# A differential-attention layer as one sequence of 128 heads: projections and norms beside the heads, both halves of the weighing together, max pieces behind them

## What is computed

```
q1, q2, k1, k2, v = heads(x, Wq1), ...          # 16 heads, 16 wide; v 32 wide
att1 = softmax(where(mask, q1 k1^T * scale, -inf))
att2 = softmax(where(mask, q2 k2^T * scale, -inf))
y = (att1 - lam * att2) v                        # per head, causal
yn = normalise y of a head and feature over time, times gn_w, plus gn_b, times gamma
out = yn Wc^T ;  x = layernorm(x + out)
```

## Time and profile before

| | us |
|---|---|
| median of 3 runs | 6893.02 (6890.95 to 6894.93) |
| the profiled execution | 6894.07 |
| its span on the core | 6892.3 |
| TensorE busy | 6310.0 (92%) |
| VectorE, ScalarE, GpSimd busy | 4158.6, 3497.0, 817.9 |
| granted TensorE clock, mean | 0.959 |

### The profile page before, as it was taken

The page is one execution under the profiler, slowest core; times in us unless marked ns, Lnnn a source line. Parts: engine busy times, 40 slices in busy tenths (PEclk is TensorE's granted clock), DMA queues, the critical chain, the costliest instruction groups (busy, mean ns, idle before and its releaser), DMA issues.

```text
span 6892.3 us, 112906 instructions
## 1 busy us (share of the span) xinstructions
PE 6310.0 (92%) x33280; PEld 2525.2 (37%) x33280; DVE 4158.6 (60%) x10732; ACT 3497.0 (51%) x6948; POOL 817.9 (12%) x1937
## 2 busy tenths in 40 slices
PE   8989999899998989989799999999999999999985
PEld 2222232223223232232244444444444444444441
DVE  5747667475675757657565565565565565556543
ACT  4646546465564645646445445544544545544532
POOL 2222122222221212222100000000000000000000
PEclk9999999999999999999899999999999999999997
DMA  2312222232222322223100000000000000000004
GB/s 58 55 38 50 44 46 49 40 53 44 46 43 47 54 42 48 38 50 54 62 10 7 13 13 7 13 13 7 13 28 10 10 13 10 10 13 10 10 7 149
DMA packets 134759, 228.62 MB, mean 33 GB/s; under 512 B 40348, under 2 KB 40476, under 8 KB 133504
## 3 DMA queue, kind: packets, MB, share of 16 engines
q1 hardware_dynamic: 134272, 222.83, 15.6%
HBM read 53.86 MB, written 33.55 MB: 13 GB/s over the span
## 4 chain that ended last, share of the span: by engine, by line
PE 71%; DVE 10%; ACT 8%; issue 8%; DMA 2%; DVEq 1%; SPq 0%; POOL 0%; ACTq 0%; POOLq 0%
PE ps L582 16%; PE ps L664 10%; PE ps L549 9%; PE ps L788 6%; PE ps L564 4%; PE ps L813 4%; PE ps L538 4%; PE ps L715 3%; PE ps L754 3%; PE ps L735 2%; ACT pt L973 2%; PE ps L723 2%; PE ps L534 2%; ACT gates L1097 1%; DVE rr L1386 1%
## 5 line engine op out<-in xcount | busy, mean ns | idle before, releaser
L973 ACT ACTIVATE pt<-ps 128x1024 f32<-128x1024 f32 (+7 forms) x2048 | 1220.2, 650 | 923.8 <-PE ps L564 921.1
L582 PE MATMUL ps<-pt,vs 128*32 128x512 f32 (+3 forms) x6144 | 1304.1, 507 | 13.1 <-POOL pt L1594 9.3
L1234 DVE CUSTOM_DVE_ANT_0 junk<-ps,causal 128x128 bf16<-128x128 f32 (+3 forms) x2048 | 981.4, 488 | 535.7 <-PE ps L549 414.7
L582 PE MATMUL ps<-pt,ones 128*32 128x512 f32 (+3 forms) x6144 | 1304.4, 507 | 0.0
L549 PE MATMUL ps<-kt,qt 96*128 96x512 bf16 (+3 forms) x3072 | 1012.1, 337 | 134.8 <-DVE mc L1234 79.5
L1238 DVE TENSOR_REDUCE mc<-ps 128x1 f32<-128x512 f32 x1024 | 705.4, 689 | 232.9 <-PE ps L549 211.4
L564 PE MATMUL ps<-qt,kt 98*128 98x512 bf16 (+3 forms) x3072 | 770.8, 335 | 36.4 <-ACT pt L973 33.1
L549 PEld LDWEIGHTS ps<-kt,qt 96*128 96x128 bf16 x3072 | 297.5, 97 | 1265.2 <-DVE mc L1234 890.2
L664 PE MATMUL ps<-wqkv,xs 128*128 128x512 f32 x1536 | 740.5, 615 | 13.5 <-DMA wqkv<-in_wqkv 13.5
L1054 ACT ACTIVATE sm<-sm,mxw 128x256 f32<-128x256 f32 (+1 forms) x1024 | 496.7, 486 | 430.6 <-DVE mxw L1394 430.2
L1594 POOL TENSOR_SCALAR_AFFINE_SELECT pt<-pt 128x256 f32<-128x256 f32 x1024 | 423.0, 413 | 1969.2 <-ACT pt L973 1969.2
(11 more groups left out here) (144 smaller groups left out, 7869.6 us busy)
## 6 DMA issues: line engine op xcount, KB each, us to landing
qt<-part SPq DMA_DIRECT2D x768, 64.0 KB, 2.4
kt<-part SPq DMA_DIRECT2D x768, 64.0 KB, 2.6
ya<-wy SPq DMA_DIRECT2D x128, 128.0 KB, 2.3
yb<-wy SPq DMA_DIRECT2D x128, 128.0 KB, 2.4
xs<-between_phases SPq DMA_DIRECT2D x32, 512.0 KB, 3.8
between_phases<-xo SPq DMA_DIRECT2D x32, 512.0 KB, 2.8
xt<-in_x SPq DMA_DIRECT2D x8, 1024.0 KB, 5.0
between_phases<-yb SPq DMA_DIRECT2D x16, 512.0 KB, 3.6
```

The lines of the kernel that those rows point to most:

```text
L582: mmi = pe.matmul(ps[32 * q:32 * q + 32, 4 + half, lo - half * 512:hi - half * 512], w, pt[:, kb % 2, i, lo:hi], start=kb == 0, stop=kb == ...
L973: act.activation(pt[:, kb % 2, i, kb * P:1024], ps[:, 2 * i:2 * i + 2, :].rearrange("p a q -> p (a q)")[:, kb * P:1024], ACT.Exp, scale=SC ...
L1234: ins = dve.tensor_tensor_reduce(out=junk[:, bank - 6, 0:w], in0=ps[:, bank, 0:w], in1=causal[:, 512 - w:512], scale=1.0, scalar=NEG, op0= ...
```

## The change

The loop over batches and the loop over groups of heads are gone in the first phase. All 128 heads (`ALL`) are one straight sequence, and pieces of head g + 2 stand beside head g across batches too. What stood between two batches' heads is spread over heads. The function `EXTRA` tells which two results (e = 0, 1) head h of batch b carries beside it: heads 6 to 9 and 14 to 16 the q/k projections of the next batch (two tiles each), heads 10 to 13 its value projections, head 1 the last two q/k tiles of its own batch, heads 2 and 3 the output projection of the batch before, head 4 its means, head 5 its variances and divisions (counted from 1; h counts from 0). PE computes result e in key block 3 + e, in two parts with a max piece behind each, into bank 2e, which scores leave free from block 4 on. The four-head groups are summed and their statistics taken in every fourth head. Value projections are now 128 columns wide (`project_v`: four key blocks by two halves of the features, 128 features a call). `xt` is double, `yb` a quarter.

In a key block, both halves of the weighing now follow each other, and pieces stand behind the scores and behind the halves: `BESIDE` is replaced by `BESIDE_S` (behind scores 0 and 1) and `BESIDE_V` (behind each half). `copy_out` of the first half moves from block 5 to 6. The diff, cut to its core:

```diff
-BESIDE = (4, 4, 3, 3, 3, 2, 2, 3)
+BESIDE_S = ((1, 1), (1, 1), (1, 1), (0, 1), (0, 1), (0, 1), (0, 1), (1, 1))
+BESIDE_V = ((0, 2), (0, 2), (0, 1), (0, 1), (1,), (1,), (0,), (0,))
...
+def EXTRA(g, e, nb):
+    b, h = divmod(g, HEADS)
+    if h == 0 and b:
+        return "qk", b, 14 + e
+    if 1 <= h <= 2 and b:
+        return "out", b - 1, 2 * (h - 1) + e
+    if h == 3 and b:
+        return "mean", b - 1, e
+    if h == 4 and b:
+        return "var", b - 1, e
+    if 5 <= h <= 8 and b + 1 < nb:
+        return "qk", b + 1, 2 * (h - 5) + e
+    if 9 <= h <= 12 and b + 1 < nb:
+        return "v", b + 1, 2 * (h - 9) + e
+    if h >= 13 and b + 1 < nb:
+        return "qk", b + 1, 8 + 2 * (h - 13) + e
+    return None, 0, 0
...
 @block.tensor
-                        for kb in range(8):
-                            steps = [(values, (g, u, kb, n)) for n in range(len(halves(kb)))]
-                            if kb < 7:
-                                steps = [(scores, (g, u, kb + 1, 0)), (scores, (g, u, kb + 1, 1))] + steps
...
-                            for n, (step, args) in enumerate(steps):
-                                step(*args)
-                                while two and k < sum(BESIDE[:kb]) + BESIDE[kb] * (n + 1) // len(steps):
-                                    if k == T_AT:
-                                        max_transpose(nxt, slot + k, parity + k)
-                                    piece(g + 2, (u + 2) % UNROLL, k, slot + slot_of(k), parity + slot_of(k))
-                                    k += 1
...
+                for kb in range(8):
+                    follow = (g, kb + 1) if kb < 7 else (g + 1, 0)
...
+                    for i in range(2):
+                        if follow[0] < ALL:
+                            scores(follow[0], follow[1], i)
+                        pieces(BESIDE_S[kb][i])
+                    if kb in (3, 4):
+                        for part_of in range(2):
+                            extra(g, kb - 3, part_of)
+                            pieces(1)
+                    for n in range(len(halves(kb))):
+                        values(g, kb, n)
+                        pieces(BESIDE_V[kb][n])
...
+            def project_v(b, n, bank, blocks):
+                j, t = n // 2, n % 2
...
+                for blk in blocks:
                     for kc in range(2):
+                        mmi = pe.matmul(ps[:, bank, blk * P:(blk + 1) * P],
+                                        xt[:, b % 2, kc, (4 * t + blk) * P:(4 * t + blk + 1) * P],
+                                        wv[:, kc, j * P:(j + 1) * P], start=kc == 0, stop=kc == 1)
...
 @block.vector
+                    for k in range(24):
+                        if k == T_AT:
+                            copy_maxima(g + 1, slot + k)
+                        if k == T_AT + 1 and g:
+                            normalise(g - 1)
+                        piece(g + 2, k, slot + slot_of(k))
+                        if k == 9 and h % 4 == 1 and g > 4:
+                            over_time(g // 4 - 1)
+                        if k == 14:
+                            extra(g, 0)
+                        if k == 18:
+                            extra(g, 1)
+                        if h % 4 == 0 and g:
+                            if k == 15:
+                                sum_group(g // 4 - 1)
+                            if 20 <= k <= 21:
+                                half_statistics(g // 4 - 1, k - 20)
+                            if k == 23:
+                                statistics(g // 4 - 1)
+                        if h == 4 and b and 21 <= k <= 22:
+                            divide(b - 1, k - 21)
```

More of the change, by code:

```diff
@@ L348, in load_x @@
             def load_x(b):
[L349 to L394, removed]
-                    load_x(b + 1)
-                for half in range(2):
-                    sp.wait_ge(norm_done, done(b * 2 + half + 1))
-                    sp.dma_start(d["sx"][bass.ds(b, 1), :, :, half * 512:half * 512 + 512].rearrange("a c p t -> p (a c) t"),
-                                 z[:, :, half * 512:half * 512 + 512]).then_inc(stored, 16)
@@ L408, in fill @@
+            values_out(ALL - 1)
+            store_x(nb - 1)
+            for half in range(2):
+                sp.wait_ge(stored[half], sent(nb))
             def fill(tile, name, l, signal):
@@ new lines, in scores, with values @@
+                mmi.then_inc(st_full, 1)
+            def values(g, kb, n):
+                half, lo, hi = halves(kb)[n]
+                if kb == 0 and g:
+                    pe.wait_ge(ev_done, done(g * 2 + (half - 1)))
+                if n == 0:
+                    if kb == 0:
+                        pe.wait_ge(vs_ready, done(g + 1))
+                    pe.wait_ge(masked, done(g * 8 + kb + 1))
+                for q in range(4):
+                    i = q % 2
+                    w = vs[:, g % 2, kb, i, :] if q < 2 else ones[:]
+                    mmi = pe.matmul(ps[32 * q:32 * q + 32, 4 + half, lo - half * 512:hi - half * 512], w,
+                                    pt[:, kb % 2, i, lo:hi], start=kb == 0, stop=kb == 4 * half + 3)
+                if n == len(halves(kb)) - 1:
+                    mmi.then_inc(pv_done, 1)
@@ L1023, in _ @@
+            copy_out(ALL - 1, 1)
+            invert(ALL - 1)
+            over_time(nb * 4 - 1)
+            for half in range(2):
+                squares(nb - 1, half)
+                inverse_deviation(nb - 1, half, 6 + half)
             act.preload_act_table_set("natural_log_exp_and_others")
@@ new lines, in extra @@
+            def extra(g, e):
+                what, b, k = EXTRA(g, e, nb)
+                if what == "qk":
+                    residual(b, k, 2 * e)
+                if what == "out":
+                    add_x(b, k, 2 * e)
+                if what == "mean":
+                    centre(b, k, 2 * e)
+            for k in range(8):
+                residual(0, k, k % 4)
+            for k in range(24):
+                piece(0, k, k)
+            two_parts(0, 23)
+            for n in range(8):
+                residual(0, 8 + n, n % 4)
+                if n == 0:
+                    copy_maxima(0, 24)
+                for k in range(3 * n, 3 * n + 3):
+                    piece(1, k, SLOTS + k)
@@ L1605, in _ @@
+            for half in range(2):
+                pool.wait_ge(stored[half], sent(nb))
             pool.memset(window[:], 0.0).then_inc(k2_ready, 1)
```

775 lines of the change are left out of this document (420 added, 355 removed).

## The result

The changed kernel takes **6727.44 us** (median of 4 runs, 6724.56 to 6733.33) against 6892.56 for the kernel before: ratio 0.9759, 95% interval 0.9744 to 0.9773. It is faster, as forecast, but by 165 us where I had 83.

The account below looks back on a forecast made before the run. TensorE, busy 92% of the span, was taken as the bound. Six inner sequences -111 us, the first -34, the last +56, front and end +2 each: net -85 on 6894.07 gives 6810 us; 8 in 10 range 6690 to 6930.

Parts of the forecast that it names:

- the length of the answer: VectorE's reading of a 384-wide masked piece was taken to start 0.56 us after TensorE's matmul of it.
- rival 1: Waits in heads smaller, VectorE keeps up: half the stalls gone gives 6590 us, a fifth 6720; chance 0.15.
- p4: Max piece 4 of a head waits for VectorE's reading of p2 until 3.03 us after the first weighing half (V).
- p5: Max piece 5 of a head waits for p3's reading until 3.87 us after the first weighing half (V).
- plain heads: Heads without extra work: 22.55 us, 2.9 more than before; nine in the last sequence.
- q/k heads: Heads with q/k projections: 3.46 us of matmul fill waits and cost 1.4, plus 0.4 at p21; 24.4 us.
- The statistics: A group's sum and statistics on VectorE in every fourth head: +1.0 us, most of it slack there.
- sixth heads: Carry a q/k projection, 24.4 us; SyncE's two stores wait some 5 us, which the longer head has to spare.
- The largest wait: Third key block: piece 9 waits for VectorE's reading of p7, behind copy, p6 and division; 1.0 us lost.
- rival 4: Pieces' waits cost 0.7 us a head more, pushed into the next head: 88 us, 6895; chance 0.10.
- rival 3: Value projections' weight loads bind: 2.7 us in 28 heads, 75 us, giving 6885; chance 0.07.
- my largest rival: Clock falls in each head's thin place, 5.6 to 8.6 us: 1.4 us a head, 176 us, 6985; chance 0.22.

Follow-up runs that it names:

- run 8: Changed kernel with the semaphore instruction that stood ahead of each masked piece on VectorE put back, nothing else: 6763.10 us, ratio 0.9810.
- run 7: Kernel before with VectorE's loops alone written out, the semaphore instruction back ahead of each masked piece and group's statistics: 6869.76 us; without that instruction 6801.66.
- run 3: Kernel before with first-phase loops of TensorE, VectorE, ScalarE and GpSimd written out, semaphore instructions ahead of single instructions gone, order untouched: 6757.18 us, ratio 0.9803.
- run 10: Changed kernel with VectorE dividing the result of the head before behind piece 8, not behind piece 6: 6639.61 us, ratio 0.9632.
- runs 3 and 4: Kernel before with four engines' first-phase loops written out: pieces in the old order 6757.18 us, in the changed kernel's new order 7035.37 us.
- run 9: Changed kernel with SyncE loading the next x directly behind the store of the result, ahead of operand loads and maxima rows: 6708.92 us, ratio 0.9734.

## Why the prediction found half of the gain

*The step that failed* is the length of the answer in the layout of the head. I let VectorE's reading begin 0.56 us after TensorE's matmul, as the earlier trace rows have it for the kernel before, and took that for execution time. In the changed kernel it is 0.37, because a semaphore instruction in VectorE's queue went with the loops. Put back, it costs the changed kernel 36 us (run 8), of the 83 that I missed.

Each part of the change by itself, from the medians, in the order in which the runs take them:

| step | us | part |
|---|---|---|
| before | 6892.6 | |
| loops written out | 6757.2 | -135 |
| one sequence, pieces as before | 6678.6 | -79 |
| the new order of pieces | 6727.4 | +49 |

*The answer.* "An order whose waits for register values are gone" stood in my text only as rival 1, at 0.15, and I put against it that the chain is made of execution times. Its figure for a fifth of the stalls gone, 6720, is near what came, but not for its reason: the cause is not the registers that I named but the semaphore instruction beside them (run 7). I took 0.56 us as a property of the chip; it was a property of this kernel's queue, and the diff removed it. In the kernel before the written-out loops bring more than that, 135 us, since there first and last heads and the ends of sequences gain too (run 3). Those parts were in my sum, which replaced each sequence whole.

*The layout of the head was right in its places and 0.2 to 0.5 us long in its sizes.* With the old answer in force, p4 falls on the laid-out time to the hundredth, p5 and all behind it come 0.22 earlier than VectorE's row suggested, and from a head's scores to its first V it is 3.23 in the changed kernel, not 3.35. Against run 8, plain heads were laid out 0.43 long, q/k heads 0.46, output heads 0.5, value heads 0.27: some 42 us of the 47 left over. The statistics were charged 16 too much and the variance heads 11; the front, the second phase (6 us shorter in run 8, where I had nothing) and the last two heads make 10 more. Against that stand the sixth heads of run 8, 34 us longer than laid out, and the mean heads, 4. These add up to 41 of the 47; the rest is not traced. The largest wait itself was right: 1.0 laid out, 0.96 measured when the division was moved (run 10). The sum was added up rightly to within its rounding (6808 written as 6810; rival 4's 6895 is 6898).

*The classes.* That the new order costs plain heads 2.4 to 2.9 us held (2.40 between runs 3 and 4, 2.52 with loops), and so the last sequence is a loss. That projections fill the waits held. Values' weight loads are hidden, as taken: rival 3 is out. The statistics were charged +1.0 and cost 0 to 0.8.

*The sixth head* was the one large error in the other direction. I named SyncE's two stores ahead of a head's operands and judged that the longer head would absorb them. The operands did come in time; the load of x behind them did not, and I had never followed that load to the projection that reads it: 4.4 to 7.4 us beyond the laid-out 24.4, six times. 2.1 of it belong to the divisions; of the laid-out 50.4 us for variance and sixth head together, run 9 has 24.0 + 25.9 = 49.9 where the clock is 1.00, so that term was right. What was missing is the x, and the clock: the five heads below 1.00 are 0.6 to 3.0 us longer than the one at 1.00, and two of them wait less than 1 us for x where it waits 2.63.

*The clock.* At 0.22 my largest rival, it did not come where I looked for it: 1.00 in 636 to 683 with PE busy 43.76 of 47 us. It came in five of the six sixth heads, at 0.88 to 0.94, and with run 9's 1.3 to 1.5 us for a head at 0.94 as the price I estimate some 11 us for all five (three of them lose about twice as much clock), in place of the rival's 176. The Trainium skill, TensorE: Matmul & The Clock Gate, § HAM oscillation, describes a kernel whose clock fell in long DMA waits between bursts of matmuls. Here it fell in the fifth sequence behind two much shorter waits, of 1.18 and 1.06 us; in the second sequence the same two waits, and 2.63 us for x behind them, left it at 1.00.

*Step by step against what I said would show it*: exps 24.4 and 22.5 apart: no, 23.76 and 21.58. PE's wait in the third key block near 1 us: yes, 0.96. Clock near 1.00 throughout: in 121 of 127 heads, not in five sixth heads and the very first head. No stretch below 85% between sequences: sixth heads are, at 78 to 86%.

*Open*: of the 135 us, 68 are the semaphore instruction and 23 the rest of VectorE's loops (run 7), TensorE's alone give none, and 44 came only with ScalarE's and GpSimd's written out as well, and GpSimd's own semaphore instructions gone; how these divide was not tried. Nor was the semaphore instruction taken out with the register operations left in, so what those cost without it is not known. The 79 us of the one sequence also hold SyncE's loop and the values' new shape. Nor is it shown whether the instruction costs by its own passage or because it changes which of the two waits stands last in front of the piece.

## What to carry to other kernels

Before a feedback time is read from a trace and laid out in a new order, look at what else stands in that queue, ahead of the instruction that answers, and whether the change removes it: 0.17 us, sixteen times a head, was worth 68 us in the old order and 36 in the new. When two banks carry a feedback, no long operation may stand between an answer and the matmul that needs it; moving one division past two short pieces gave 0.97 us of 21.6. And follow each moved load to its first reader, not only to the queue that it passes.

## What the runs showed that I had not expected

- A semaphore instruction on VectorE ahead of a piece that TensorE waits for costs 0.17 us of the answer (0.55 against 0.38) and, sixteen times a head, 0.41 us a head (19.67 against 19.26), though no row of the profile shows it. The Trainium skill, Perfetto Trace Analysis, § DVE / Act Engine Instruction, says that an instruction's decoding and waiting lie ahead of its reported start; the rows here agree in so far as the cost shows only as a later start.
- Written-out loops on TensorE change nothing (0.9998), though a register operation stood ahead of nearly every matmul group.
- The granted clock can go either way on the same instructions. In the sixth head of the second sequence it stays at 1.00 with TensorE 79% busy for 29 us and idle places up to 2.63 us; in the five that follow it falls to 0.88 to 0.94, in two of them (the fifth and seventh sequence) with no idle place above 1.2 us ahead of the fall. In run 9, with no wait for x at all, it falls in two of the six, and a head at 0.94 takes 1.3 to 1.5 us more. In the earlier trace rows it was 0.84 at 73% and 0.80 at 81%. What tells these apart is not settled by these runs.
